# First-layer loads, edge sorting and turns in one block, with the score end reordered

## The reference

```python
h = jnp.maximum(_layernorm(x, axis=-1), 0.0)
x = x + _L0_gnn_ref(h, L0_gnn_W, adj, L0_gnn_bias)       # layer 0
h = jnp.maximum(_layernorm(x, axis=-1), 0.0)
x = x + _L1_gnn_ref(h, adj, ...)                         # two products with batch norms
h = jnp.maximum(_layernorm(x, axis=-1), 0.0)
x = x + _L2_gnn_ref(h, adj, ...)                         # two graph products, four LSTMs
h = jnp.maximum(_layernorm(x, axis=-1), 0.0)
x = x + _L3_gnn_ref(h, L3_gnn_W_lin, L3_gnn_W_val, L3_gnn_a, L3_gnn_W_out, adj, L3_gnn_src, L3_gnn_dst)
```

```python
h = jnp.einsum('bjf,kfo->kbjo', x, W)
out = einsum('ij,bjo->bio', adj_0, h[0]) + einsum('ij,bjo->bio', adj_1, h[1]) + einsum('ij,bjo->bio', adj_2, h[2])
```

## Time and profile before

| what | value |
|---|---|
| three runs, median | 1301.64 us (1301.43 to 1303.98) |
| the profiled execution's own time | 1302.56 us |
| its span | 1300.8 us |
| PE busy | 1233.4 us (95%) |
| DVE busy | 1018.0 us (78%) |
| ACT busy | 869.3 us (67%) |
| POOL busy | 327.2 us (25%) |

### The profile page before, as it was taken

How to read it: one execution, slowest core, us unless ns; L and a number is a source line. 1 busy time by engine, 2 the same in 40 slices (tenths; PEclk the granted TensorE clock), 3 DMA queues, 4 the chain that set the end, 5 groups by cost and what they waited for, 6 DMA issues and landing times.

```text
span 1300.8 us, 23507 instructions
## 1 busy us (share of the span) xinstructions
PE 1233.4 (95%) x7340; PEld 1024.8 (79%) x7340; DVE 1018.0 (78%) x2039; ACT 869.3 (67%) x1649; POOL 327.2 (25%) x738
## 2 busy tenths in 40 slices
PE   2999999999999998899999999999999899988998
PEld 1989996664388887689778887988897778768998
DVE  4788766996768885998788878887876699986664
ACT  1666657867758886877687768777766677752332
POOL 3577761000057440000000000000000566642331
PEclk9999999999999999999999999999999999998999
DMA  8000000000031110000000000002100300001112
GB/s 302 1 0 0 0 0 0 0 1 0 0 131 66 71 57 1 1 1 1 1 1 1 1 1 1 1 1 81 49 1 1 130 1 2 1 2 41 66 74 82
DMA packets 14475, 38.02 MB, mean 29 GB/s; under 512 B 1856, under 2 KB 3904, under 8 KB 13120
## 3 DMA queue, kind: packets, MB, share of 16 engines
q1 hardware_dynamic: 13008, 36.31, 7.3%
q10 hardware_dynamic: 1392, 0.74, 0.2%
HBM read 20.27 MB, written 16.78 MB: 28 GB/s over the span
## 4 chain that ended last, share of the span: by engine, by line
PE 52%; DVE 5%; ACT 2%; issue 1%; POOL 1%; POOLq 0%; DVEq 0%; ACTq 0%
PE bank L966 7%; PE bank L967 7%; PE bank L968 7%; PE bank L1546 5%; PE bank L981 4%; PE bank L1334 4%; PE bank L1346 4%; PE bank L977 4%; PE bank L978 4%; PE bank L1536 2%; PE bank L1554 2%; ACT gates L996 1%; PE bank L1318 1%; PE bank L1239 1%; DVE Y L1051 1%
## 5 line engine op out<-in xcount | busy, mean ns | idle before, releaser
L996 ACT ACTIVATE gates<-bank,lstm_bias 128x512 f32<-128x512 f32 (+1 forms) x504 | 301.9, 637 | 101.4 <-PE bank L981 88.3
L150 ACT ACTIVATE l_h<-X,nmr,rstd 128x128 f32 (+1 forms) x512 | 209.9, 483 | 56.7 <-POOLq L144 36.0
L966 PE MATMUL bank<-lstm_node_hi,Wih_hi 128*128 128x512 f32 (+1 forms) x408 | 149.5, 366 | 0.0
L967 PE MATMUL bank<-lstm_node_hi,Wih_lo 128*128 128x512 f32 (+1 forms) x408 | 148.9, 365 | 0.0
L968 PE MATMUL bank<-lstm_node_lo,Wih_hi 128*128 128x512 f32 (+1 forms) x408 | 148.8, 365 | 0.0
L119 POOL TENSOR_TENSOR l2r_sum<-l2r_st 128x8 f32<-128x8 f32 x16 | 4.2, 265 | 528.8 <-DVE l2r_st L100 528.8
L977 PE MATMUL bank<-lstm_hid_hi,Whh_hi 128*128 128x512 f32 (+1 forms) x288 | 104.1, 362 | 3.9 <-DVE lstm_hid_hi L1056 3.8
L981 PE MATMUL bank<-lstm_hid_lo,Whh_hi 128*128 128x512 f32 (+1 forms) x288 | 106.8, 371 | 0.0
L978 PE MATMUL bank<-lstm_hid_hi,Whh_lo 128*128 128x512 f32 (+1 forms) x288 | 103.1, 358 | 0.0
L1001 ACT ACTIVATE gates<-lstm_cell 128x512 f32<-128x512 f32 (+1 forms) x144 | 83.7, 581 | 20.8 <-DVE lstm_cell L1043 20.4
L968 PEld LDWEIGHTS bank<-lstm_node_lo,Wih_hi 128*128 128x128 f32 x408 | 77.1, 189 | 11.7
(11 more groups left out here) (247 smaller groups left out, 3279.8 us busy)
## 6 DMA issues: line engine op xcount, KB each, us to landing
X<-in_x SPq DMA_DIRECT2D x8, 1024.0 KB, 14.6
x_spill<-X SPq DMA_DIRECT2D x32, 256.0 KB, 2.0
X<-x_spill SPq DMA_DIRECT2D x2, 4096.0 KB, 12.7
out<-X SPq DMA_DIRECT2D x32, 256.0 KB, 2.0
w_raw<-in_WihT SPq DMA_DIRECT2D x1, 1024.0 KB, 6.4
w_raw<-in_WhhT SPq DMA_DIRECT2D x1, 1024.0 KB, 8.9
W<-in_L_W ACTq DMA_DIRECT2D x1, 192.0 KB, 4.9
rows<-in_rows ACTq DMA_DIRECT2D x1, 128.0 KB, 3.9
```

Source lines behind the costliest of these rows:

```text
L150: last = act.activation(h[:, j, :], k.X[:, bass.ds(b0, TB), :][:, j, :], ACT.Relu, bias=k.nmr[:, bass.ds(b0, TB)][:, j:j + 1], scale=k.rst ...
L966: pe.matmul(out, hi, x_high, start=True, stop=False)
L967: pe.matmul(out, lo, x_high, start=False, stop=False)
L996: act.activation(gate_of(it, g), k.bank[4 * s + g][:, 0:it.N], ACT.Tanh if g == GATE_G else ACT.Sigmoid, bias=k.lstm_bias[:, it.p - 1, g:g ...
```

## The change

1. `stage_setup`, `stage_edges` and `stage_layer0` become one block, `stage_first`. X is loaded right behind the two copies of adj, in pieces of one turn, one turn and then two turns; edge lists and last-layer weights come behind X. The 16 turns are written out one after the other; no engine has a loop there.
2. The work of the other two stages is placed between the turns, by numbers: `DEG, SPREAD, L3, FLOAT, RANK, PERM, SORTED, ADJ, SUM, TURN, SHARE = 0, 3, 3, 4, 5, 6, 7, 8, 9, 10, 11`. Its products all go to one bank, the one in which slot 0's output is made; TensorE waits for that bank before a product, and for its reader before the slot's output. The casts and copies into row, col, sorted_row, DTr, S1 and same move from VectorE to ScalarE.
3. ScalarE normalises the first two tiles of the hidden stage inside the block. The last batch of layer-norm coefficients moves from this block to the hidden stage's block.
4. The Ln and the Sigmoid behind it move to the start of `stage_gcn_out`.
5. In the scores' last turns, the high halves (ScalarE) and low halves (GpSimd) of the first two value tiles are made a turn earlier, the table of Exp is loaded a turn earlier by an activation with an unread result, the Exp goes behind the transposed copies, and TensorE's turn_back stands between the two tiles' products. VectorE weighs and makes the first weighted tile ahead of the second tile's M. In `Attend` the chunks' linear term and turn_in come two steps later.

```diff
+    turns_in = [1, 1] + [2] * ((n_it - 2) // 2)
...
+            for c, n in enumerate(turns_in):
+                rows = slice(first * S * TB, (first + n) * S * TB)
+                sp.dma_start(X[:, rows, :], d["x"][:, rows, :]).then_inc(x_in[c], 16)
+                first += n
...
-            with pool.Fori(0, n_it - AHEAD) as i:
-                turn(i, True)
-            for i in range(n_it - AHEAD, n_it):
-                turn(i, False)
+            for i in range(n_it):
+                if i + AHEAD < n_it:
+                    x_ln.coefficients(pool, i + AHEAD)
+                if i < n_it - 1:
+                    ln.coefficients(pool, i)
...
+                if i == SORTED:
+                    pe.wait_ge(updated[0], i)
+                    pe.wait_ge(permed, EC)
+                    for n in range(2):
+                        for c in range(EC):
+                            last = pe.matmul(spare[:, n * E:(n + 1) * E], colbc[:, n, c, :], perm[:, c, :], start=c == 0, stop=c == EC - 1)
+                    last.then_inc(sorted_done, 1)
...
+                if i == DEG:
+                    dve.reduce_sum(rs[:, 0:1], adj[:, :], mybir.AxisListType.X)
+                    dve.reduce_sum(rs[:, 1:2], k.adjT[:, :], mybir.AxisListType.X)
...
+            for t in range(S):
+                ln.wait(act, t, 0)
+                normalise_tile(act, k, k.hidden_h[t], t * TB).then_inc(k.hidden_h_done, 1)
...
-            stay_awake(pe, k, psT[0], 26)
+            stay_awake(pe, k, psT[0], 10)
...
+        @block.gpsimd
+        def _(pool):
+            k.l0_ln.coefficients(pool, n_it - 1)
...
-            stay_awake(pe, k, k.bank[6], 8)
             steps(pe, step)
...
+            act.activation(e.log_w[:, :], e.log_w[:, :], ACT.Ln).then_inc(logged, 1)
+            act.wait_ge(logged, 1)
+            act.activation(unread[:, :], k.zero[:, :], ACT.Sigmoid)
...
-            if i == n_it - 1:
-                at.sm.turn_back(pe, 0)
             for s in range(S):
+                if i == n_it - 1 and s == S - 1:
+                    at.sm.turn_back(pe, 0)
...
-            if due(t, 10):
-                sm.linear_term(pe, due(t, 10))
-            if due(t, 9):
-                sm.turn_in(pe, due(t, 9))
+            if due(t, 8):
+                sm.linear_term(pe, due(t, 8))
+            if due(t, 7):
+                sm.turn_in(pe, due(t, 7))
```

More of the change, by code:

```diff
@@ L13 @@
+import itertools
 from contextlib import ExitStack
@@ L205, in _ @@
-            sp.dma_start(e.a_sign[:, :], d["a"].rearrange("(o a) -> o a", o=1).partition_broadcast(P)
[L206 to L220, removed]
+            first = 0
@@ L323, in normalise @@
                     act.activation(h_hi[s][:, :, :], h[s][:, :, :], ACT.Copy).then_inc(hi_ready[s], 1)
-            def turn(i, ahead):
+            normalise(0)
+            for i in range(n_it):
+                if i == SORTED:
+                    act.wait_ge(sorted_done, 1)
+                    act.activation(sorted_row[:, :, :], spare[:, :].rearrange("p (n e) -> p n e", n=2), ACT.Copy).then_inc(sorted_in, 1)
+                if i == TURN:
+                    act.wait_ge(turned, 1)
+                    act.activation(e.S1[:, :, :], spare[:, 0:E].rearrange("p (c n) -> p c n", c=EC), ACT.Copy).then_inc(S1_in, 1)
+                if i == SHARE:
+                    act.wait_ge(shared, 1)
+                    act.activation(e.same[:, :, :], spare[:, :].rearrange("p (c x) -> p c x", c=EC), ACT.Copy).then_inc(same_in, 1)
                 for s in range(S):
@@ L341, in _ @@
+            for i in range(n_it):
+                extra(i)
                 for s in range(S):
@@ new lines, in _ @@
+            dve.wait_ge(adj_in, 32)
+            dve.wait_ge(cst, 2)
+            dve.tensor_tensor(tmp[:, :], adj[:, :], k.ident[:, :], ALU.mult).then_inc(diag_in, 1)
+            x_stats(0)
+            dve.wait_ge(masks, 2)
+            split_float32(dve, A12T[:, :, :], A_hi[:, :, :], A_lo[:, :, :], A_ready, 1).then_inc(A_ready, 1)
+            dve.wait_ge(diag_done, 1)
+            dve.tensor_copy(diag_bc[:, :], spare[:, 0:P]).then_inc(diag_done, 1)
+            x_stats(1)
+            for s in range(S):
+                h_low(0, s)
@@ L434, in step @@
             def step(t, s):
-                if there(t + 1):
-                    if since(t + 1, S):
-                        act.wait_ge(Z_done, t + 1 - S + 1)
+                if isinstance(t, int) and t == 2:
+                    for q in range(S):
+                        k.l0_ln.wait(act, q, n_it - 1)
+                if there(t + 1) and since(t + 1, S):
+                    act.wait_ge(Z_done, t + 1 - S + 1)
                     normalise_tile(act, k, h[(s + 1) % S], (t + 1) * TB).then_inc(h_done, 1)
@@ L1375, in on_vector @@
                 last.then_inc(R["M"][s], 1)
+                if i == n_it - 1 and s == 0:
+                    at.sm.weigh(dve, 0)
+                if i == n_it - 1:
+                    at.weighted(dve, s)
             if i == n_it - 2:
@@ L1380, in on_vector @@
                 at.sm.subtract_max(dve, 0)
-            if i == n_it - 1:
-                for t in range(2):
-                    at.weighted(dve, t)
             for s in range(S):
```

454 lines of the change are left out of this document (217 added, 237 removed).

## The result

The changed kernel takes 1282.57 us (median of 4 runs, 1282.38 to 1284.02) against 1302.19 in the runs beside it: a ratio of 0.9852, with a 95% interval of 0.9839 to 0.9866. It is 19.6 us faster; 33.7 were forecast.

What follows compares the result with a forecast made beforehand. TensorE, busy 95% of the span, bounds the kernel; GpSimd paces layer 0's loop. Savings 17.6 + 0.5 + 6.4 + 9.2 = 33.7 from 1302.56 give 1268.9, less 0.9 for the median: 1268 us, range 1257 to 1279.

Steps and rivals of the forecast that it cites:

- The turns: Layer 0's turns, written out with other stages' work between them: net 0.5 us saved, from 9 lost to 7 saved.
- Each brings two waits: TensorE's six inserted steps in layer 0 wait for slot 0's add into X and the shared bank's reader; both covered.
- The "slower" rival: Layer 0's start: TensorE's clock stays at 1.2 GHz, 8.6 us more per turn; 1320 us with six such turns; chance 0.03.
- GpSimd's pace: Layer 0: GpSimd, held by VectorE's adds, paces 12 turns at a mean of 9.85 us, 0.3 less than before.
- The inserted work adds up: Layer 0: VectorE's 8.8 us and TensorE's 3 lengthen the turns, instead of the 3.1 counted; 1277 us; chance 0.2.
- Its sign: A TensorE wait for Z0 over 1 us in layer 0's turns 1 and 4 to 10 supports the inserted-work rival.
- GpSimd stops pacing: Layer 0: VectorE's adds miss GpSimd's batches, turns fall to TensorE's own 9.37 us, 5.8 less; 1262 us; chance 0.2.
- The start: Before layer 0: X's first piece lands at 6.5 us, first normalise at 12.8 instead of 30.42; 17.6 us saved.
- Into the hidden stage: Layer 0's end to the first W1 product: 5.1 us for 11.50, 6.4 saved; the moved batch fits narrowly.
- Ln and Sigmoid: Moved to the start of `stage_gcn_out`, into ScalarE's idle time: nothing gained, 0 to 0.5 us lost.
- Score end: End of the scores: TensorE's Exp and `add_linear` waits shrink; 9.2 us saved, from 5 to 10.3.
- The wait for `turn_in`: At the scores' end, TensorE waits 0.8 us for turn_in ahead of project(0).

Runs made afterwards that it cites:

- filled waits: Changed kernel with 14 products without use ahead of each of the three TensorE steps that waited (turns 3, 7, 8): 1277.64 us; with 28: 1284.64 us.
- the other two traces: Changed kernel with X's first piece ahead of adj and ScalarE's loads held back, 1282.45 us; changed kernel with the old entry to the hidden stage, 1290.70 us.
- the late steps: Changed kernel with all six inserted TensorE steps a whole turn or more behind the work that feeds them: 1269.78 us.
- the bias run: Changed kernel with its inserted TensorE steps moved later, and without VectorE's bias add into X in layer 0: 1266.38 us.

## Why the prediction was wrong

**The turns: the step that failed.** Right was that the inserted steps are small and that the banks' readers cost nothing. Wrong was "Each brings two waits", one for the add into X and one for the reader of the bank. There is a third, for the step's own input, and for three of the six it is made among VectorE's last instructions of the turn before. The prediction looked at what each step overwrites and who reads its result, and did not ask who feeds it. It had the number: VectorE ends 2.51 us behind TensorE at the layer's end, with nothing behind its statistics. Those 2.5 and VectorE's own 0.3 to 0.6 for the input make up most of the 3.0 to 3.7 measured. With the steps a turn later, 12.8 of the 14.6 us of error are gone, and with only two of the inputs made earlier 10.0.

**What one such wait costs** is more than its length, and the prediction had no price for it. Of the 16.9 us in the trace of the changed kernel, 10.1 are waiting in the three turns, and 5.9 come from TensorE's clock, which fell towards the lower level behind each wait (filled waits); with the ninth turn as the other two traces have it, the clock's part is 4.6. The last 0.9 is what is left; it holds the steps' own time and VectorE's wait for the transposes; the runs do not part them. The "slower" rival had the right mechanism in the wrong place: it feared the clock at layer 0's start, where only the first 4 us of products were slow (four transposes in 1.09 us at 16.51, 0.70 at 20.54), and not behind a wait that the change itself makes.

**GpSimd's pace.** Walked at 9.85 us a turn, and 3.1 us added for the inserted work, it came out at 10.02 with the late steps. So 150.26 us for fifteen turns against 150.17: written out, with the edge work between, the layer is neither faster nor slower. The forecast of 0.5 saved is then off by only 0.6, but in part by luck, since the turns don't run as walked. GpSimd was to pace twelve of them; ScalarE waits for it in eight of them with the late steps (0.18 to 1.35 us), and in two in the changed kernel. And with GpSimd freed a turn is 9.68 on average, not the 9.37 that was put for TensorE's own. That GpSimd is held by VectorE's adds follows from the rule of the Trainium skill ("SBUF — State Buffer", section "Who interferes with whom") that a VectorE instruction with two inputs in SBUF contends with a GpSimd instruction that reads SBUF. It agrees with the bias run, 0.34 us a turn; that run also shortens VectorE, so it does not show the lock alone.

**The rivals.** "The inserted work adds up" came nearest in time (1277), for the wrong reason: the same work in the same turns, with its inputs earlier, is 10 us faster. Its sign, a TensorE wait for Z0 over 1 us, came in two turns, at 1.20 and 1.19 us. "GpSimd stops pacing" happened in ten of its twelve turns in the changed kernel, where the three long ones let GpSimd catch up; made to happen in all, on the late steps, it is worth 5.0 by the turns and 3.4 in the kernel's time, not 5.8, since TensorE's inserted steps count then.

**The start** was 1.9 short. The term that failed is the landing of X. 417 GB/s was taken from the full stream, but between 4 and 6 us the changed kernel's queues move 103 and 158 GB/s, with adj ahead of the piece and ScalarE's small loads beside it. Issued first, and with those held back, it lands 3.4 us sooner. The rest (1.82, 4.17 and 0.30) came as forecast: 8.46 to 14.72 is 6.26.

**Into the hidden stage** 6.75 for 6.4: right. The moved batch did fit: ScalarE waits 1.58 for it (at 197.56), and TensorE never. **Ln and Sigmoid** 0.1 for 0: right. **Score end** 10.5 for 9.2: the mechanism was right, and the range named 10.3 as its upper end, for a faster scan. The scan did run faster, by 1.10, and that is most of the 1.3 (before, then after):

```profile
1153.43 1.79 DVE L1450 TENSOR_TENSOR_SCAN sm_m<-reset,sm_r 128x256 f32<-128x256 f32 x1
1143.98 0.69 DVE L1462 TENSOR_TENSOR_SCAN sm_m<-reset,sm_r 128x256 f32<-128x256 f32 x1
```

Before, GpSimd makes the low halves at 1152.17 to 1154.67, across the start of the scan; in the changed kernel they are done at 1139.92. The run with the old score end has it back (1.78). With the faster scan the exponential is kept 1.1 us earlier than the sum had it. The wait for `turn_in` was forecast at 0.8 and is 0.82.

## What to carry to other kernels

An instruction put at the head of an engine's turn has three waits: what it overwrites, who reads it, and who makes its input. Ask for each how far its maker trails at that point, and put a turn between maker and user where the work isn't urgent. Price a new wait on TensorE with what the clock does behind it, and when a wait's place moves, move the products that fill it. An engine's own pace is known only once its inserted work is in it.

## What the runs showed of the hardware

In the changed kernel TensorE's clock fell towards the lower level (0.66, 0.66 and 0.50 in the five microseconds behind) after each of the three waits of 3.0 to 3.7 us, in the midst of a layer in which it was busy before and after, and cost 1.5, 1.5 and 2.8 us of turn. The last of these varies from one execution to the next: with the same code the turn took 16.30, 15.06 and 14.99. A shorter wait can do it too, and not each time: 1.77 us was followed by 0.50 in one trace and by 1.00 in another. Filled with products of no use for 3.29 us, the three waits cost little beyond the fill and what waiting is left: 12.92, 13.68 and 13.46, against 9.10, 10.41 and 9.53 for the same turns where the step doesn't wait.

Small loads beside others cost a lot in the first microseconds. adj's second copy, issued behind the first piece of X at 1.73, landed at 4.81 with ScalarE's loads held back and at 7.83 with two of them (W0 and the rows, 0.32 MB) beside it. The piece of X itself, 0.5 MB, was awaited until 8.46 us behind adj and beside all of ScalarE's loads; issued first, it had landed by 4.43 and 5.13 in these two runs. The stream holds what is issued behind it: W0, 192 KB, took 13.2 us to land instead of 3.0.
